# Differential attention: order of the two halves of a unit on TensorE, ScalarE and VectorE, and order of GpSimd's three steps

## The reference, cut to what matters

```python
q = _rope((x @ Wq).reshape(b, s, H, 2 * D));  k, v likewise with 4 KV heads, each repeated 4 times
qd, kd = q.reshape(b, s, H, 2, D), k.reshape(b, s, H, 2, D)
energy = jnp.einsum('bqhad,bkhad->bahqk', qd, kd)
energy = jnp.where(causal, NEG, energy)
scores = jax.nn.softmax(energy / np.sqrt(D), axis=-1)
diff = scores[:, 0] - lam * scores[:, 1]
diff = jnp.where(causal, NEG, diff)
diff = jax.nn.softmax(diff, axis=-1)
att = jnp.einsum('bhqv,bvhd->bqhd', diff, v)
```

## Time and profile before

| what | value |
|---|---|
| median of 3 runs | 2949.13 us (2944.26 to 2956.90) |
| the profiled execution: its time, its span | 2956.03 us, 2954.3 us |
| busy in the span: TensorE, VectorE, ScalarE, GpSimd | 84%, 67%, 58%, 29% |
| mean granted TensorE clock | 0.907 of full speed |
| differential attention, first to last L1360 to L1474 | about 1257 to 1952 us of the span |
| L1360, L1445, L1474, L1410 busy | 380.7, 372.6, 208.3, 191.9 us |
| L1401: GpSimd idle before it, for ScalarE | 282.4 us of 304.8 |

### The profile page before, as it was taken

The page is one execution under the profiler, slowest core; times in us unless marked ns, Lnnn a source line. Parts: engine busy times, 40 slices in busy tenths (PEclk is TensorE's granted clock), DMA queues, the critical chain, the costliest instruction groups (busy, mean ns, idle before and its releaser), DMA issues. The chain is left out here.

```text
span 2954.3 us, 68881 instructions
## 1 busy us (share of the span) xinstructions
PE 2488.9 (84%) x25231; PEld 1675.3 (57%) x25320; DVE 1982.2 (67%) x4308; ACT 1712.4 (58%) x3452; POOL 865.9 (29%) x1229
## 2 busy tenths in 40 slices
PE   8878877888888788988888888878999688899998
PEld 3433336643333266545555445557887466888888
DVE  5488886677787576788788888864333345576652
ACT  2588864324454543387788788853222334576778
POOL 2233334121111141355555555520000213232223
PEclk9999988978899888989999999998999777899999
DMA  4533302244233022522040222004000558622210
GB/s 166 151 72 71 71 0 95 91 113 59 36 51 44 14 93 88 139 32 30 11 50 2 31 30 30 1 7 171 1 1 12 95 128 175 89 29 32 47 31 8
DMA packets 282130, 177.16 MB, mean 60 GB/s; under 512 B 204736, under 2 KB 241616, under 8 KB 279760
## 3 DMA queue, kind: packets, MB, share of 16 engines
q1 hardware_dynamic: 272640, 164.54, 26.6%
q10 hardware_dynamic: 9168, 8.41, 1.2%
HBM read 113.84 MB, written 54.66 MB: 57 GB/s over the span
## 5 line engine op out<-in xcount | busy, mean ns | idle before, releaser
L1360 ACT ACTIVATE ad_e<-ps,ad_nm 128x1024 f32<-128x1024 f32 (+7 forms) x512 | 380.7, 745 | 115.6 <-DVE ad_nm L1445 109.9
L1445 DVE TENSOR_REDUCE ad_nm<-ps 128x1 f32<-128x1024 f32 (+7 forms) x512 | 372.6, 752 | 46.4 <-PE ps L1293 36.0
L670 ACT ACTIVATE ab_e<-ps 128x512 f32<-128x512 f32 (+3 forms) x384 | 167.1, 490 | 199.5 <-PE ps L585 198.4
L1291 PE MATMUL ps<-fd_k_st,fd_q_st 96*128 96x512 bf16 (+3 forms) x768 | 218.4, 344 | 57.4 <-ACT ad_e L1360 52.4
L1474 DVE CUSTOM_DVE_ANT_0 ad_t<-ad_e,ad_rz 128x128 f32<-128x128 f32 (+7 forms) x256 | 208.3, 813 | 41.1 <-POOL ad_e L1410 24.6
L1410 POOL TENSOR_SCALAR ad_e<-ad_e,ad_c 128x128 f32<-128x128 f32 (+7 forms) x256 | 191.9, 750 | 19.2 <-DVE ad_c L1462 17.9
L1306 PE MATMUL ps<-ident,ad_t 128*128 128x128 f32 x1152 | 172.8, 278 | 26.8 <-ACT ad_prT L1370 13.1
L1886 POOL TENSOR_TENSOR st_it_low<-st_it,st_it_high 128x256 fp32r<-128x256 f32 x128 | 98.5, 782 | 324.0 <-ACT st_it_high L2149 318.2
L1401 POOL TENSOR_SCALAR_AFFINE_SELECT ad_e<-ad_e 128x128 f32<-128x128 f32 x256 | 90.3, 353 | 304.8 <-ACT ad_e L1360 282.4
L1370 ACT ACTIVATE ad_prT<-ps 128x128 f32<-128x128 f32 (+7 forms) x256 | 166.5, 650 | 21.4 <-PE ps L1314 21.2
L675 ACT ACTIVATE aa_e<-ps 128x1024 f32<-128x1024 f32 (+1 forms) x192 | 150.8, 836 | 35.3 <-PE ps L585 32.7
(11 more groups left out here) (393 smaller groups left out, 7146.6 us busy)
## 6 DMA issues: line engine op xcount, KB each, us to landing
scr_a<-pa_parts SPq DMA_DIRECT2D x24, 512.0 KB, 2.8
fa_q_st<-scr_a SPq DMA_DIRECT2D x24, 512.0 KB, 7.7
split<-f_split SPq DMA_DIRECT2D x16, 768.0 KB, 3.9
fd_q_st<-scr_d SPq DMA_DIRECT2D x48, 256.0 KB, 8.0
g_w<-split SPq DMA_DIRECT2D x8, 1536.0 KB, 17.5
scr_d<-pd_parts SPq DMA_DIRECT2D x20, 384.0 KB, 2.7
st_w_first<-split ACTq DMA_DIRECT2D x5, 1536.0 KB, 8.3
fa_k_st<-scr_a SPq DMA_DIRECT2D x24, 256.0 KB, 8.5
```

Source lines behind the costliest of these rows:

```text
L670: act.activation(e[:, u % ER, h, lo:QB], m.ps[:, n4(u, h) % 3, lo:QB], ACT.Exp, scale=scale).then_inc(s_read[0], 1)
L1291: last = pe.matmul(m.ps[:, bank, 0:n], q_st[:, b, 2 * h + s, t * P:(t + 1) * P], k_st[:, b, s, cc * QB:cc * QB + n], start=True, stop=True)
L1360: act.activation(e[:, u % EB, s, 0:L], src, ACT.Exp, bias=nm[:, u % EB, s:s + 1], accum_out=z[:, u % EB, s:s + 1]).then_inc(exped[s], 1)
L1445: dve.tensor_reduce(nm[:, u % EB, s:s + 1], src, AX.X, ALU.max, negate=True).then_inc(maxed[s], 1)
```

## The change

In short rows Q1, E1 and M1 of a unit move up, behind Q0, E0 and M0 of the same unit. In long rows they stay where they were. VectorE does C ahead of X, in short and in long rows alike (the two entries for `mix` are together the one that stood there). GpSimd does Sc first, then Sp, and Mk one unit later than before, last in its slot.

```diff
+    def of_rows(short, fn):
+        def run(i, u):
+            if (place(u)[2] < 4) == short:
+                fn(i, u)
+        return run
...
-            pipelined(pe, [(0, score(0)), (5, turn), (0, score(1)), (6, value(0)), (7, value(1)), (8, value(2)),
+            pipelined(pe, [(0, score(0)), (0, of_rows(True, score(1))), (5, turn), (0, of_rows(False, score(1))), (6, value(0)), (7, value(1)), (8, value(2)),
                            (10, turn_back)], PER, ITERS, lead=16)
...
-            pipelined(act, [(0, exps(0)), (5, softmax), (0, exps(1)), (9, copy_out), (11, keep_result)],
+            pipelined(act, [(0, exps(0)), (0, of_rows(True, exps(1))), (5, softmax), (0, of_rows(False, exps(1))), (9, copy_out), (11, keep_result)],
                       PER, ITERS, lead=16)
...
-            pipelined(pool, [(4, spread_top), (0, mask), (2, scale_second)], PER, ITERS, lead=16)
+            pipelined(pool, [(2, scale_second), (4, spread_top), (1, mask)], PER, ITERS, lead=16)
...
-            pipelined(dve, [(0, maxima(0)), (3, mix), (1, coefficients), (0, maxima(1))], PER, ITERS, lead=16)
+            pipelined(dve, [(0, maxima(0)), (0, of_rows(True, maxima(1))), (1, coefficients), (3, of_rows(True, mix)),
+                            (3, of_rows(False, mix)), (0, of_rows(False, maxima(1)))], PER, ITERS, lead=16)
```

## The result

The changed kernel takes 3034.69 us, the median of four runs (3022.63 to 3040.68), and the kernel before takes 2946.70 beside it (2939.97 to 2956.90). The ratio is 1.0277, with a 95% interval of 1.0240 to 1.0314: slower by 88 us. The forecast was 2987 us, at most 3014. The sign was right. The size was not, for the time lies outside the range, and the meeting of VectorE and GpSimd that takes place is not the one that was priced.

The account below looks back on a forecast made before the run. VectorE was taken to bound long rows, no engine to be full in short ones, TensorE fullest at t = 0. Terms 13 + 26 - 11 + 11 = 39 us; 38 added to the 2949 median gave 2987 us, range 2938 to 3014.

Parts of the forecast that it names:

- C ends, X starts at once, Sc is released only 0.21 us after C: Long rows, slot with C: X goes first and GpSimd's Sc stands still for the whole X.
- The forecast meeting: Long rows: GpSimd's second Sc of a pair holds up VectorE's next X, 0.4 us a pair, 26 us in all.
- C's wait for E1: Long rows: with C ahead of X, VectorE waits 0.2 us a pair for E1's sum, 13 us in all.
- Short rows: t = 1 to 3: early M1 and Q1 save 1.4 us a pass, 11 us; bounds 0 and 29.
- The ring: Short rows: M0, M1, C, X, Sc, Sp, T, V, Q0 chained over two slots, 3.8 us for two units at t = 2.
- The faster rival: Short rows reach VectorE's busy time, long-row gaps absorb E1's wait: -22 us, 2927 us; chance 0.13.
- its floor: Short rows: VectorE's busy time as the limit, allowing a gain of at most 3.6 us a pass, 29 us.
- The seam: Long to short rows, 7 times: T starts 1.5 us later behind Q1, 11 us in all; bounds 2 to 11.
- The rival of the clock: At each seam TensorE idles and its clock falls: 10 to 20 us on top, about 3003 us; chance 0.12.

Follow-up runs that it names:

- e5: The kernel before with only GpSimd's new order (Sc, Sp, Mk a unit later), X still ahead of C: 2964.71 us, ratio 1.0050.
- e1: The kernel after, with VectorE doing X ahead of C again: 2980.89 us, ratio 1.0121.
- e3: The kernel after, with GpSimd's Sc also waiting until X of the same slot is over: 3013.44 us, ratio 1.0225.
- e7: As e6, but the first short unit of a pass keeps the old order of its halves: 2926.29 us, ratio 0.9916.
- e6: The kernel before with only Q1, E1 and M1 of short rows early; old VectorE and GpSimd orders of X, C, Sc, Sp, Mk: 2953.67 us, ratio 1.0022.
- e9: As e7, with T's matmul on zeros left out for units of 1024 keys: 2921.28 us, ratio 0.9878.
- e4: The kernel before with only C ahead of X on VectorE, in all rows: 2987.91 us, ratio 1.0131.
- e8: The kernel after, with M1 of long rows placed between C and X: 2980.55 us, ratio 1.0082.

## Why the prediction was wrong

**The step that failed** is "C ends, X starts at once, Sc is released only 0.21 us after C". Sc was taken from a row. X was not: no row of the prediction has an X directly behind C, and no reason is given for "at once". Measured, X starts 0.23 us after C, 0.03 later than Sc. From that step followed who stands still (in the forecast GpSimd, which has time; in fact VectorE, which has none), which pair meets, and how long. In the kernel after, the meeting costs 0.82 us a pair at t = 7 and 42 us in all, where 26 was forecast for another meeting.

**The forecast meeting** is real (e5, e1), at 0.5 us a pair where 0.4 was given, but it costs time only at t = 6 and 7, and was seen only where X stands ahead of C. The value of t = 7 should not have been taken for all row lengths.

**C's wait for E1** was forecast at 13 us and is right as a wait, 0.2 us. C's place costs 28 us in long rows nonetheless (e3), for the same missing hand-over stands in it as idle time: 0.24 us directly and 0.1 of lost overlap. It was taken as part of no term. Directly behind C the trace of before has only maxima, which start 0.08 us before C's end and so gave no hint.

**Short rows** were given -11 us for t = 1 to 3; t = 2 and 3 gave -3, and t = 1 took 3, so nothing was gained. The ring that the forecast drew had one meeting more in it: X of 384 keys has a mean of 807 ns in the kernel after and 616 before. What early halves can give is seen in e7, with the old orders of GpSimd and VectorE: 0.98 and 1.52 us at t = 2 and 3. GpSimd's new order on top of them (e1 against e6) takes 0.71, 1.20 and 0.75 us at t = 1, 2 and 3. The faster rival wanted "that Sc gets its turn before X in short rows". That came true, 0.21 against 0.23 us after C, and did not help, since X then stood still for Sc and the new orders kept the ring; VectorE reached its floor only where neither of them is in place (e6, e7, e9).

**The seam** was forecast 1.5 us longer by Q1 ahead of T and measured at 1.54. But it is 3.5 us longer in the kernel after. Beside the 1.54 stand 1.34 for the meeting of X and Sc with C's place, which the forecast left to long rows. The 0.7 that remain were not measured by themselves. The clock is the likely cause, but prices need not add up here: in e3, without the meeting, the seam takes 12.4 us at full clock and 12.9 to 13.1 at the low one.

**The rival of the clock** came true in part. It was priced at 10 to 20 us. Where one kernel shows a seam at both levels, the low clock costs 1.1 to 1.2 us (e6) or 0.5 to 0.6 (e3); for the seven seams of the kernel after, all low, that gives an estimate of 4 to 9 us.

**The sum.** In the terms of the forecast (39 us for long rows, -11 for short ones, 11 for the seam) the stage shows 69, 0 and 24. (The forecast adds 38 to the median where its terms make 39; that is 1 us.) Alone, the three parts change the stage by +33.5 (e4), +10.6 (e5) and -4.7 us (e6), together +39.4, which is the forecast's own +39. Made together they cost 94. By medians the long rows of e4 and e5 add up to 42 us, and the kernel after has 70 there; the remaining excess is in short rows and the seam. So the forecast summed parts, two of which act on one path that VectorE and GpSimd share, and the 55 us between the two sums are the interaction of the parts. That the sum of single costs agrees with the forecast is luck, since its terms differ: C's place was given 13 us and takes 33.5, GpSimd's order 26 and takes 10.6, the early halves 0 (11 less 11) and take -4.7.

**What stays open.** What lies outside the stage is the same program in all kernels and yet took 2254 us (kernel after) to 2280 us (e9) in the profiled executions, 2267 in the kernel before. So the shares above are those of the stage, and totals and stages need not agree to better than some 10 us. Why e6's seam falls to the low clock in four passes and not in three was not settled.

## What to carry to other kernels

When two engines use memory by turns, find out who reaches it first before pricing either edit: here Sc was 0.03 us ahead of X, and the full engine stood still in place of the one with spare time. An instruction that reads PSUM, put behind the one that releases the other engine's SBUF work, avoided the meeting at t = 7 (e8). Do not add up single prices of edits that meet on such a path. An edit that shifts halves of a unit should be looked at where its loop changes size: keeping one unit of 32 in its old order turned no gain (e6) into a gain of 0.8% (e7).

## What the hardware showed that had not been expected

A tiny VectorE instruction (C's last, 0.16 us, 128 x 2 elements) is followed by X only after a hole of 0.23 to 0.24 us, in the kernel after, in e3 and in e4. The same kind of C is followed by a maximum on PSUM after 0.01 us (e8). So the hole belongs to what stands ahead of X, and not to C alone. The trace of the kernel after points at its cause: between C and X the queue of VectorE holds three instructions that only handle semaphores (L388 twice, at 1729.1 and 1729.2, and L1480 at 1729.3, 0.05 us long), for X waits for five semaphores and raises one before it starts. Between C and a maximum in e8 stands none or one of them, and in e8 X's three lie under the maximum. That they make the hole is not shown by a run; one with fewer waits ahead of X would tell. The X and Sp that were blocked show no idle time for it: they show a longer record, 2.03 for 1.15 us on VectorE and 1.20 for 0.37 on GpSimd. The busy time of VectorE that rose with the same instructions was a wait in disguise. Last, 1.97 us of idle time on TensorE at the same place of the program was followed by the low clock in four passes of e6 and not in three others.
